# A two-batch expert kernel: the second layer's block sums go from GpSimd to VectorE, and six pieces change place in the queues

## What is computed

```python
s0 = relu(x @ swi[0]) @ swo[0]; s1 = relu(x @ swi[1]) @ swo[1]
eo = relu(x @ wi[type]) @ wo[type]
w  = softmax(relu(concat(eo[:, 0], s0[:, 0], s1[:, 0]) @ g1) @ g2)   # batch's first token
x  = x + eo * w[0] + s0 * w[1] + s1 * w[2]
x  = x + x @ W[category] + b[category]
```

## Time and profile before

| | |
|---|---|
| median of 3 runs | 1956.5 us |
| the profiled execution | 1956.29 us, span 1954.4 us |
| TensorE (PE) busy | 1933.9 us, 99% |
| VectorE (DVE) busy | 1343.6 us, 69% |
| ScalarE (ACT) busy | 981.7 us, 50% |
| GpSimd (POOL) busy | 402.1 us, 21% |
| TensorE's mean granted clock | 0.997 |

### The profile page before, as it was taken

The page is one execution under the profiler, slowest core; times in us unless marked ns, Lnnn a source line. Parts: engine busy times, 40 slices in busy tenths (PEclk is TensorE's granted clock), DMA queues, the critical chain, the costliest instruction groups (busy, mean ns, idle before and its releaser), DMA issues.

```text
span 1954.4 us, 25279 instructions
## 1 busy us (share of the span) xinstructions
PE 1933.9 (99%) x8510; PEld 1597.6 (82%) x8510; DVE 1343.6 (69%) x1508; ACT 981.7 (50%) x1438; POOL 402.1 (21%) x283
## 2 busy tenths in 40 slices
PE   7999999999999999999999999999999999999999
PEld 6888888887888888888888888888878888888887
DVE  8888888898576556565655545589975656555566
ACT  5766766756454334444554344456555433344342
POOL 3234224322211111331111111122321111111120
PEclk9999999999999999999999999999999999999999
DMA  6876777768876666786776676578777776656642
GB/s 219 300 292 249 292 279 295 278 242 304 277 256 217 204 204 215 266 293 211 261 258 204 193 224 209 189 278 295 267 279 257 239 228 221 216 182 211 224 156 97
DMA packets 192321, 468.29 MB, mean 240 GB/s; under 512 B 17476, under 2 KB 58436, under 8 KB 185924
## 3 DMA queue, kind: packets, MB, share of 16 engines
q1 hardware_dynamic: 192196, 466.69, 69.8%
HBM read 319.82 MB, written 146.80 MB: 239 GB/s over the span
## 4 chain that ended last, share of the span: by engine, by line
PE 73%; DVE 2%; DMA 1%; issue 1%; ACT 1%; SPq 0%; ACTq 0%; DVEq 0%
PE ups L1555 35%; PE rps L1555 35%; PE aps L1555 3%; DMA XT<-xT_kept 1%; DVE WD L1173 0%; DVE XL L1157 0%; DVE HL L1186 0%; DVE HT L737 0%; ACT XH L843 0%; ACT HH L938 0%; DVE ACC L1205 0%; DVE XT L1512 0%; ACT WD L874 0%; DVE XL L1518 0%; PE aps L1654 0%
## 5 line engine op out<-in xcount | busy, mean ns | idle before, releaser
L1555 PE MATMUL ups<-XH,WU 128*128 128x512 f32 x2660 | 878.0, 391 | 14.1 <-issue 4.4
L1555 PE MATMUL rps<-HH,WD 128*128 128x512 f32 x2672 | 876.5, 389 | 0.6 <-ACT rps L953 0.6
L1555 PEld LDWEIGHTS ups<-XH,WU 128*128 128x128 f32 x2660 | 501.7, 189 | 123.0 <-issue 11.0
L1555 PEld LDWEIGHTS rps<-HH,WD 128*128 128x128 f32 x2672 | 501.3, 188 | 105.4 <-DVE HL L1186 1.3
L1555 PE MATMUL rps<-HL,WD 128*128 128x512 f32 x1336 | 519.7, 389 | 0.0
L1555 PE MATMUL ups<-XL,WU 128*128 128x512 f32 x1330 | 519.3, 390 | 0.0
L737 POOL TENSOR_TENSOR HT<-hid 128x512 f32<-128x512 f32 x96 | 133.2, 1388 | 1316.8 <-PE rps L1555 1298.2
L1186 DVE TENSOR_TENSOR HL<-HT,HH 128x1024 fp32r<-128x1024 f32 x240 | 290.2, 1219 | 9.6 <-ACT HH L938 5.1
L1208 DVE SCALAR_TENSOR_TENSOR ACC<-rps,gw,ACC 128x1024 f32<-128x1024 f32 x126 | 161.6, 1282 | 196.6 <-PE rps L1555 196.3
L1555 PEld LDWEIGHTS rps<-HL,WD 128*128 128x128 f32 x1336 | 251.0, 188 | 52.1
L1555 PEld LDWEIGHTS ups<-XL,WU 128*128 128x128 f32 x1330 | 250.6, 188 | 51.5
(11 more groups left out here) (129 smaller groups left out, 1521.7 us busy)
## 6 DMA issues: line engine op xcount, KB each, us to landing
WU<-wu_kept SPq DMA_DIRECT2D x448, 256.0 KB, 3.5
WD<-wd_kept SPq DMA_DIRECT2D x224, 512.0 KB, 3.3
wd_kept<-WD SPq DMA_DIRECT2D x112, 512.0 KB, 3.5
wu_kept<-WU SPq DMA_DIRECT2D x31, 1024.0 KB, 4.9
wu_kept<-WU SPq DMA_DIRECT2D x31, 768.0 KB, 4.5
sums_kept<-ACC SPq DMA_DIRECT2D x28, 512.0 KB, 5.4
MB<-sums_kept SPq DMA_DIRECT2D x28, 512.0 KB, 5.7
XS<-in_x_dram SPq DMA_DIRECT2D x21, 512.0 KB, 5.8
```

The source lines that it names most:

```text
L1555: ins = pe.matmul(dst, stationary[a], moving[c], start=start and j == 0, stop=stop and j == 2, skip_group_check=True)
```

## The change

`down_sums` is taken off GpSimd and put on VectorE. Its early part for step N comes at the end of the loop before, behind `made(m, 5)`; its late part comes inside step d, behind `hidden_low(d, 2)` and ahead of `made(m, 0)`. For step 0 the early part stands ahead of the loop. In the start steps, on ScalarE token parts 4 and 5, the seventh product's copy, `chain(a)` and `first_down_product(d)` come earlier, and on VectorE `second(0)` and token part 4 go ahead of the hidden sums and part 5 behind them. The fourth `gate_partial` of steps 8, 9, 32 and 33 goes behind `hidden_low(N, 0)`. At the end of step 46 two hidden sums of step 47 are made ahead of an `add_sum`, and the tail's order follows. In the diff `more` is m < 47.

```diff
--- before.py
+++ after.py
@@ -771,22 +771,6 @@
                 pool.wait_ge(s_S0, 3)
                 pool.tensor_tensor(SR[:, 3, :], A12, SR[:, 1, :], ALU.subtract).then_inc(s_S0, 1)
 
-            def down_sums(N, late):
-                k = 4 * PREP[N]
-                A11, A12, A21, A22 = (PDR[:, q, :, :] for q in range(4))
-
-                if late:
-                    pool.tensor_tensor(PDS[:, 2, :, :], A11, A21, ALU.subtract).then_inc(s_Sd, 1)
-                    pool.wait_ge(s_Sd, k + 2)
-                    pool.tensor_tensor(PDS[:, 3, :, :], A12, PDS[:, 1, :, :], ALU.subtract).then_inc(s_Sd, 1)
-                    return
-                pool.wait_ge(s_pd, 16 * (PREP[N] + 1))
-                if PREP[N] > 0:
-                    pool.wait_ge(s_wld, PRODUCTS * PREP[N])
-                pool.tensor_tensor(PDS[:, 0, :, :], A21, A22, ALU.add).then_inc(s_Sd, 1)
-                pool.wait_ge(s_Sd, k + 1)
-                pool.tensor_tensor(PDS[:, 1, :, :], PDS[:, 0, :, :], A11, ALU.subtract).then_inc(s_Sd, 1)
-
             def category_identity(b):
                 pool.wait_ge(s_wc, 16 * (b + 1))
                 for k in range(KD):
@@ -801,9 +785,7 @@
             pool.wait_ge(s_ident, 1)
             hidden_sum(pool, 0, 0, 0)
             hidden_sum(pool, 0, 0, 1)
-            down_sums(0, False)
             hidden_sum(pool, 0, 0, 2)
-            down_sums(0, True)
             for m in range(STEPS):
                 N, d = m + 1, m
                 hidden_sum(pool, d, 0, 3)
@@ -815,14 +797,10 @@
                 if N < STEPS:
                     hidden_sum(pool, N, 0, 0)
                     hidden_sum(pool, N, 0, 1)
-                if prepared(N):
-                    down_sums(N, False)
                 if N < STEPS:
                     hidden_sum(pool, N, 0, 2)
                 if m in (19, 20):
                     ahead_sum(pool, m - 17, 3)
-                if prepared(N):
-                    down_sums(N, True)
                 if m in (STEPS_SUPER, 3 * STEPS_SUPER):
                     category_identity(m // (2 * STEPS_SUPER))
 
@@ -1059,17 +1037,19 @@
                     first_product(a)
                 if start:
                     token_high(s + 1, 4)
-                if d >= 0:
-                    hidden_high(d, 3)
-                if more:
+                    token_high(s + 1, 5)
                     seventh_product(a)
+                hidden_high(d, 3)
+                if more and not start:
+                    seventh_product(a)
+                if start:
+                    chain(a)
                 made(m - 1, PRODUCTS - 1)
-                if d >= 0:
-                    hidden_high(d, 2)
                 if start:
-                    token_high(s + 1, 5)
+                    first_down_product(d)
+                hidden_high(d, 2)
                 second(0)
-                if more:
+                if more and not start:
                     chain(a)
                 if d >= 0:
                     hidden_high(d, 6)
@@ -1077,7 +1057,7 @@
                     token_high(s + 1, 6)
                 if more:
                     relu_11(a)
-                if d >= 0:
+                if not start:
                     first_down_product(d)
                 if d > 0 and super_of(d) % 2 == 1 and rel == 1:
                     scale_sums(d)
@@ -1326,6 +1306,23 @@
                 dve.wait_ge(s_Su, k + 3)
                 dve.tensor_tensor(PUS[:, 3, :], A12, PUS[:, 1, :], ALU.subtract).then_inc(s_Su, 1)
 
+            def down_sums(N, late):
+
+                k = 4 * PREP[N]
+                A11, A12, A21, A22 = (PDR[:, q, :, :] for q in range(4))
+
+                if late:
+                    dve.tensor_tensor(PDS[:, 2, :, :], A11, A21, ALU.subtract).then_inc(s_Sd, 1)
+                    dve.wait_ge(s_Sd, k + 2)
+                    dve.tensor_tensor(PDS[:, 3, :, :], A12, PDS[:, 1, :, :], ALU.subtract).then_inc(s_Sd, 1)
+                    return
+                dve.wait_ge(s_pd, 16 * (PREP[N] + 1))
+                if PREP[N] > 0:
+                    dve.wait_ge(s_wld, PRODUCTS * PREP[N])
+                dve.tensor_tensor(PDS[:, 0, :, :], A21, A22, ALU.add).then_inc(s_Sd, 1)
+                dve.wait_ge(s_Sd, k + 1)
+                dve.tensor_tensor(PDS[:, 1, :, :], PDS[:, 0, :, :], A11, ALU.subtract).then_inc(s_Sd, 1)
+
             def first_up_low(k):
                 dve.wait_ge(s_whu, k + 1)
                 dve.tensor_tensor(WD[:, k, 0, 1, :], PF[:, PLAIN_WEIGHTS[k], :], WD[:, k, 0, 0, :].bitcast(F32),
@@ -1366,6 +1363,7 @@
             up_low(2, 1)
             down_low(0, 0)
             down_low(0, 1)
+            down_sums(0, False)
             for m in range(STEPS - 1):
                 N, d = m + 1, m
                 a, b = 2 * N, 2 * N + 1
@@ -1388,7 +1386,7 @@
                         gate_partial(s // 2, 2, 2 * i - 1)
                     if m == STEPS - 3 and i >= 3:
                         add_tokens(i - 3)
-                    if m >= 0 and s % 2 == 0 and rel in (8, 9) and 1 <= i <= KD:
+                    if s % 2 == 0 and rel in (8, 9) and 1 <= i < KD:
                         gate_partial(s // 2, rel - 8, i - 1)
 
                 def made(m, i):
@@ -1407,23 +1405,26 @@
 
                 if start:
                     token_low(s + 1, 3)
-                if d >= 0:
-                    hidden_sum(dve, d, 1, 0)
-                    hidden_sum(dve, d, 1, 1)
-                    hidden_sum(dve, d, 1, 3)
+                    second(0)
+                    token_low(s + 1, 4)
+                hidden_sum(dve, d, 1, 0)
+                hidden_sum(dve, d, 1, 1)
+                hidden_sum(dve, d, 1, 3)
+                if start:
+                    token_low(s + 1, 5)
                 if m > 0 and prepared_half(a):
                     up_low(a, 1)
                 if prepared_half(b):
                     up_sums(b)
                 made(m - 1, PRODUCTS - 1)
                 hidden_low(d, 1)
-                second(0)
-                if start:
-                    token_low(s + 1, 4)
-                    token_low(s + 1, 5)
+                if not start:
+                    second(0)
                 if d >= 0:
                     hidden_sum(dve, d, 1, 2)
                     hidden_low(d, 2)
+                if prepared(d):
+                    down_sums(d, True)
                 made(m, 0)
                 if d > 0 and slice_of(d) == 0 and super_of(d - 1) % 2 == 0:
                     first_token(super_of(d - 1) // 2, net_of(d - 1))
@@ -1477,6 +1478,8 @@
                         mix_low(ms, c)
                 block_22(b)
                 hidden_low(N, 0)
+                if s % 2 == 0 and rel in (8, 9):
+                    gate_partial(s // 2, rel - 8, KD - 1)
                 mix(1, 1)
                 second(5)
                 if gating:
@@ -1486,8 +1489,13 @@
                 block_21(b)
                 out_part(1, 1)
                 made(m, 5)
+                if prepared(N):
+                    down_sums(N, False)
                 if end:
                     token_low(s + 1, 2)
+                if m == STEPS - 2:
+                    hidden_sum(dve, N, 1, 0)
+                    hidden_sum(dve, N, 1, 1)
                 second(6)
                 mix(1, 2)
                 if gating:
@@ -1519,11 +1527,9 @@
                                   ALU.subtract).then_inc(s_tlo, 1)
 
             pair = ups_all[:, 0:2, :]
-            hidden_sum(dve, t0, 1, 0)
-            hidden_sum(dve, t0, 1, 1)
-            add_sum(t0 - 1, 6)
             hidden_sum(dve, t0, 1, 3)
             hidden_low(t0, 1)
+            add_sum(t0 - 1, 6)
             hidden_low(t0, 3)
             hidden_sum(dve, t0, 1, 2)
             last_add(1, 0, rps[0], 0, True)
```

## The result

| | before | after |
|---|---|---|
| median | 1956.3 us (4 runs) | 2004.2 us (4 runs, 1997.4 to 2004.4) |
| ratio | | 1.0239 (1.0227 to 1.0251) |
| the profiled execution | 1956.29 us, span 1954.4 | 2004.42 us, span 2002.6 |
| PE, VectorE, GpSimd busy | 1933.9, 1343.6, 402.1 us | 1952.1, 1359.8, 294.1 us |

A forecast was written before the change was run, and what follows sets the result against it. PE, busy 99% of the span, was taken to bound the kernel. Late-sum stalls 23.4, clock 3.2, start steps 1.9 and 1.9, beginning 0.9, gate partial -1.1 and tail -0.9 gave +29.3 us: 1985.7 us, range 1973 to 2001.

The forecast's parts named there:

- The late sums' stall: Prepared steps: up(a,4) waits for chain(a) behind the late sum, 2.1 us in step 6's pattern; sum 23.4 us.
- VectorE can't be there sooner: Step 6: PE releases add_sum(m-1,5), then VectorE works without idle time up to the late sums' place.
- the cover: Loop's end, ahead of add_sum(m,5): the early sums add 1.4 us, room is 2.1 us, so cost 0.
- the gate partial's -1.1: Step 33: the partial no longer stands ahead of block_22, so PE's wait and slow start go; -1.1 us.
- The clock: Falls to 1.2 GHz behind the new stalls: two taken at 1.6 us each, 3.2 us, bounds 0 and 21.
- the sign of a wrong clock term: Profile after: more than four new stretches at granted clock 0.50 would show the clock term wrong.
- rival B: The clock falls at most of the stalls, 21 instead of 3.2 us: about 2003 us; chance 0.10.
- The start steps: Steps 11 and 35: the old stall goes, up(a,6) waits 4.2 and 3.5 us; +1.9 us each.
- The beginning: Up to step 0: earlier gains shrink to 0.7 us, the 3.9 us stall may bring a fall; +0.9 us.
- The tail: Kernel's end: two hidden sums fill VectorE idle time; the wait at 1911.90 and slow start go; -0.9 us.
- Rival A: Faster: VectorE gains more from GpSimd's silence than the sums cost, no up(a,4) waits; 1944 us; chance 0.06.
- Rival D: No change: the waits for the sums are met in time; 1956 us; chance 0.03.

The follow-up runs named there:

- e7: The kernel before, with only the two late sums on VectorE and the early ones on GpSimd: 2002.7 us, ratio 1.0238.
- e4: The kernel before, with down_sums alone moved to VectorE at the changed kernel's places, none of the other moves: 2005.5 us, ratio 1.0249.
- e9: The changed kernel with the fourth gate_partial back in its old place in second(4): 2001.3 us, ratio 1.023.

## Why the prediction was right in kind and wrong in size

*The late sums' stall* was right: place, queue and size. 1.91 us were counted from VectorE to PE, 1.97 came (292.05 to 294.01 in step 6, 412.06 to 414.03 in step 9, 455.96 to 457.93 in step 10). What I left out is the slow start behind a wait (first matmul 0.50 us, the next one 0.34 us later instead of 0.23); with the 0.06 it makes the 0.2 us by which step 6 is longer than forecast (40.38 against 40.2). The step "VectorE can't be there sooner" was shown by moving the sums one place.

*The step that failed* is the cover that I had read in step 6 and carried to steps 9, 10, 33 and 34. It stands in two places: "The early sums ... Added 1.4, room 2.1: cost 0", and the stalls of these four steps, which count PE's wait at up(a,4) (6.7 us) and nothing behind it. With the gate partial's -1.1 they were put at 5.6 us and cost 16.9, which is 11.3 of the 18.9 us missing. What an edit takes from one step of a pair it can give to the other, so they are added (us more than before the change, each from one profiled execution):

| us | steps 9 and 10 | steps 33 and 34 |
|---|---|---|
| forecast | 3.6 | 2.0 (3.1 without the gate partial) |
| late sums alone (e7) | 6.9 | 5.8 |
| all sums (e4) | 9.0 | 7.9 |
| changed kernel, gate partial back (e9) | 9.1 | 8.0 |
| changed kernel | 9.3 | 7.5 |

The late sums alone cost 5.9 us more than forecast, the early ones 4.4 instead of 0 (3.3 of it two falls), and the gate partial's new place gave 0.15 instead of 1.1. What the runs show in place of the cover is a VectorE without room. In step 9 before the change the second `block_22` was ready 0.4 us before its product's turn (414.79 us against 415.2). With the late sums alone VectorE does their 1.2 us of work ahead of it and waits three times for high parts from ScalarE (0.18, 0.74 and 0.56 us), and from 430.4 us to that `block_22` it has no idle time; PE waits 2.40 us. In step 10 the room of 2.1 us wasn't there even before the change: `add_sum(9,5)` stood 1.8 us into the step, with no idle time before it.

```profile
421.02 1.21 DVE L1205 TENSOR_TENSOR ACC<-rps,ACC 128x1024 f32<-128x1024 f32 x1
```

In the changed kernel the first early sum meets GpSimd's `hidden_sum` (1.79 us, the upper bound that I had written down and not used), and the `add_sum` starts at 445.17, 3.1 us into step 10, instead of 0.2 in step 6. VectorE, then GpSimd:

```profile
441.53 1.28 DVE L1153 TENSOR_TENSOR WD<-PDR,WD 128x512 fp32r<-128x512 f32 x2
442.73 1.79 DVE L1322 TENSOR_TENSOR PDS<-PDR 128x512 f32<-128x512 f32 x1
444.56 0.69 DVE L1324 TENSOR_TENSOR PDS<-PDS,PDR 128x512 f32<-128x512 f32 x1
445.17 1.22 DVE L1185 TENSOR_TENSOR ACC<-rps,ACC 128x1024 f32<-128x1024 f32 x1
```

```profile
442.28 1.69 POOL L737 TENSOR_TENSOR HT<-HT 128x512 f32<-128x512 f32 x1 [4.14 <-PE rps L1561]
```

The late sum, `chain` and up(a,4) are late by as much. That the early sum takes 1.79 us where the earlier trace rows have 0.69 for its like agrees with the Trainium skill, "SBUF — State Buffer", section "Who interferes with whom": whichever engine gets the shared pair of ports first keeps it for the whole instruction, and the other waits. In the trace GpSimd's instruction ends at 443.97 and the early sum 0.55 us later.

*The clock.* Two falls were counted among the plain stalls and three came; their price, 1.6 us, was right (42.00 against 40.38). But behind the long stalls of steps 10, 11 and 35 the clock stays at 0.50 (1.2 GHz) for twice as long, 6.8 instead of 3.4 us. Step 10 and step 11, in stretches of 3.4 us (columns of rows 2, clock third from the right):

```profile
456.10:459.50 3.40, 1.57 (x4) 1.29 (x5) 2.49 (x4) 2.74 (x5) 0.00 (x0) 0.51 0.17 67
459.50:462.90 3.40, 3.40 (x10) 2.63 (x9) 2.75 (x5) 3.40 (x7) 0.00 (x0) 0.50 0.28 116
462.90:466.30 3.40, 3.40 (x17) 2.80 (x16) 2.68 (x4) 1.43 (x3) 0.00 (x0) 0.99 0.88 341
507.30:510.70 3.40, 2.72 (x6) 2.15 (x7) 3.40 (x5) 2.62 (x4) 0.00 (x0) 0.51 0.49 179
510.70:514.10 3.40, 3.40 (x9) 2.64 (x8) 3.40 (x5) 0.94 (x2) 0.00 (x0) 0.50 0.60 204
```

By the distances between matmuls this costs 2.5 us in step 10, 3.0 in 11 and 2.9 in 35, and step 34 has a fall of 1.7. All matmuls at reduced clock outside the beginning cost 13.5 us more than before; I had counted 4.8 (two falls in plain steps, two in start steps, one removed). So of the 18.9 us missing 8.7 are clock, nearly half of it in steps 10 and 34, where it is also part of the miss above. Six stretches at 0.50 are new outside the beginning (steps 2, 3, 10, 32, 34, 35), more than the four that I had named as the sign of a wrong clock term. The limit "between 1.87 and 2.15 us of idle" that rival B rested on isn't there: 1.97 us had a fall behind them (step 4 of the run with the wait only), 2.20 us had none (step 11 of the run with the sums together). B's 2003 us is next to the measured time by luck. It had 21 us of clock, at thirteen stalls, and nothing of what steps 9, 10, 33 and 34 cost without it.

*The start steps* came as counted but for the clock: up(24,4) and the chain are on time, up(24,6) waits for `block_22` to 507.98, 20.38 us into the step (20.7 forecast). For step 35 the +1.9 doesn't follow from the terms beside it (3.5 - 1.9 + 1.6 = 3.2 us; with 0.57 us of idle at 1440.99, which also go and which I left out, 2.7); 3.5 came. Step 11:

```profile
507.98 0.80 PE L1561 MATMUL ups<-XH,WU 128*128 128x512 f32 x1 [3.90 <-DVE hid L1207]
```

*Step 23* cost 1.0 us where I had put 0: the token parts ahead of the hidden sums make `block_22` late there too (17.1 us into the step, due at 16.3); in the versions that keep the old order there it lasts 38.08 us. *The beginning* cost 1.5 (0.9 forecast): up(2,4) started at 49.13 (48.65 forecast) and the fall came. *The tail* gave 1.1 (0.9). *Steps 9 and 33* cost 1.9 and 0.8 (1.0 and -0.1). Their stall was as counted, and the wait in 33 went, but in both steps several waits of 0.1 to 0.15 us, some 23 to 25 us into the step, cost another 0.7 us; the clock is 1.00 there, and what makes these products late I didn't take apart.

*Rival A* fell as argued: relief from GpSimd's collisions lies before PE's release, and the late sum stood at 11.08 us, not 2.1 us sooner. *Rival D* fell too: ScalarE waits 6.67 us for the late sum.

| us | forecast | measured |
|---|---|---|
| plain stalls, steps 1 to 8 and 32, two falls among them | 19.9 | 23.3 |
| steps 9 and 33 | 0.9 | 2.6 |
| steps 10 and 34 | 4.7 | 14.3 |
| steps 11 and 35 | 3.8 | 6.6 |
| step 23 | 0 | 1.0 |
| beginning and tail | 0 | 0.4 |
| sum | 29.3 | 48.2 |

## What to carry to other kernels

Before work is moved between engines, look for who waits for its result and what stands behind that waiter in its queue; the price is read there (1.1 us per step for one place), not in the moved work's duration, and a kernel can lose 2.5% by a wait that adds no instruction. A cover read in one step holds for steps of that pattern only: look at the step with the most extra work, take off the delay that the change itself brings into it, and add neighbouring steps up before crediting or blaming one edit. Where PE was busy without a gap, price each new stall twice, bare and with the fall of the clock behind it: here it came behind some of the 2-us stalls and behind all of about 4 us, where it cost 1.6 to 3.0 us more.

## What the runs showed of the hardware that I had not expected

With 2.01 us of idle ahead of it, a stretch of matmuls ran at the full or at half the granted clock in different executions of the same kernel, at the same step. Of its first profile's stalls of 3.7 to 4.3 us three had 6.8 us at 0.50 with or behind them and two 3.4, where those of 2 us had 3.4 or none. Over the profiles of all twelve runs, from step 1 on, 21 of 50 stalls with 1.9 to 2.2 us of idle had such a stretch, 5 of 14 with 2.4 to 3.3 us, and all 24 with 3.5 us or more. And work that collides costs by where it meets the other engine: the same early sum took 0.69 us ahead of step 6 and 1.79 ahead of step 10:

```profile
278.89 0.69 DVE L1322 TENSOR_TENSOR PDS<-PDR 128x512 f32<-128x512 f32 x1
```
